# Turning the attention output: TensorE transposes against a DMA transpose of fp16 parts, with the batch loop written out

## The reference

```python
xn = layernorm(x)                                # over the 512 features
q, k, v = split(xn @ Wqkv.T + b)                 # 16 q, 8 k heads of 128; v in 4 groups of 256
p1 = softmax(causal(q[..., 0, :] @ k[..., 0, :].T / sqrt(128)))
p2 = softmax(causal(q[..., 1, :] @ k[..., 1, :].T / sqrt(128)))
o  = (p1 - lam * p2) @ v                         # 8 heads of 256 features
o  = o * rsqrt(mean(o * o) + 1e-5) * subln_w * (1 - 0.8 + 0.6 * exp(-0.3))
s  = concat(o) @ out_w.T + out_b                 # 2048 -> 512
g  = silu(mxfp4(xn) @ mxfp4(w_ffn).T + b_ffn)    # blocks of 32 rounded to 4 bits
out = x + s * g
```

## Time and profile before

| | |
|---|---|
| median of 3 runs | 1853.18 us (1851.12 to 1853.88) |
| profiled execution, span | 1849.4 us |
| PE busy | 1678.1 us (91%) |
| DVE busy | 1267.4 us (69%) |
| ACT busy | 965.0 us (52%) |
| POOL busy | 712.8 us (39%) |
| a batch of the loop (same piece of work, 839.0 less 623.35 us) | 215.65 us |
| data moved by DMA | 42.34 MB |

### The profile page before, as it was taken

One profiled execution on the slowest core, in us unless ns is written; L12 is line 12 of the kernel. 1 busy time (PEld: TensorE's weight loads), 2 busy tenths in 40 slices (PEclk: granted clock), 3 DMA queues, 4 the chain that ended last, 5 costly groups with the idle time before them and its releaser, 6 DMA issues.

```text
span 1849.4 us, 32092 instructions
## 1 busy us (share of the span) xinstructions
PE 1678.1 (91%) x10577; PEld 1036.1 (56%) x10577; DVE 1267.4 (69%) x2829; ACT 965.0 (52%) x2642; POOL 712.8 (39%) x1442
## 2 busy tenths in 40 slices
PE   3567999999899998999989998899989999999988
PEld 2344565556555565556655566555655566555654
DVE  4678888458864688548884588646885488844782
ACT  4655566336643466436663366435664356633661
POOL 2224553236422463225532364224632255323243
PEclk7879999999999999999999999999999999999999
DMA  7200000100000000100001000000001000000001
GB/s 256 91 24 1 1 2 5 48 18 2 1 30 29 13 1 1 42 24 7 1 14 41 18 1 1 30 24 18 1 1 42 24 7 1 7 24 24 1 1 40
DMA packets 20708, 42.34 MB, mean 23 GB/s; under 512 B 1682, under 2 KB 2228, under 8 KB 20532
## 3 DMA queue, kind: packets, MB, share of 16 engines
q1 hardware_dynamic: 20532, 40.13, 6.4%
HBM read 31.74 MB, written 8.39 MB: 22 GB/s over the span
## 4 chain that ended last, share of the span: by engine, by line
PE 40%; DVE 23%; issue 17%; ACT 11%; POOL 7%; DVEq 1%; DMA 0%; POOLq 0%; SPq 0%; ACTq 0%
PE ps L420 11%; PE ps L422 11%; PE ps L421 11%; ACT pp L656 7%; DVE negmax L924 5%; DVE qkv L881 2%; DVE ps L922 2%; DVE coef L937 2%; ACT qkv L634 2%; PE ps L476 1%; PE ps L544 1%; POOL res L1119 1%; DVE ebias L927 1%; DVE v L891 1%; POOL res L1122 1%
## 5 line engine op out<-in xcount | busy, mean ns | idle before, releaser
L656 ACT ACTIVATE pp<-ps,ebias,ssc 128x384 f32<-128x384 f32 (+3 forms) x512 | 312.1, 614 | 292.0 <-DVE ebias L927 225.5
L420 PE MATMUL ps<-xT,wqkv 128*128 128x512 f16 x768 | 296.0, 385 | 10.0 <-DVE qkv L881 5.9
L421 PE MATMUL ps<-xT,wqkv 128*128 128x512 f16 x768 | 295.6, 385 | 0.0
L422 PE MATMUL ps<-xT,wqkv 128*128 128x512 f16 x768 | 295.1, 384 | 0.0
L702 ACT ACTIVATE junk<-ps 128x256 bf16<-128x256 f32 x256 | 97.9, 383 | 274.7 <-PE ps L422 274.6
L420 PE MATMUL ps<-qkv,pT 128*128 128x256 f16 x640 | 174.4, 272 | 56.4 <-issue 40.4
L924 DVE TENSOR_REDUCE negmax<-ps 128x2 f32<-128x256 f32 (+3 forms) x256 | 211.1, 825 | 8.8
L913 DVE SCALAR_TENSOR_TENSOR res<-ps,small,obias 128x512 f32<-128x512 f32 x32 | 24.0, 751 | 255.5 <-PE ps L422 255.5
L420 PE MATMUL ps<-wout,heads 128*128 128x512 f16 x512 | 194.0, 379 | 0.0
L421 PE MATMUL ps<-wout,heads 128*128 128x512 f16 x512 | 194.0, 379 | 0.0
L422 PE MATMUL ps<-wout,heads 128*128 128x512 f16 x512 | 194.0, 379 | 0.0
(11 more groups left out here) (150 smaller groups left out, 3768.1 us busy)
## 6 DMA issues: line engine op xcount, KB each, us to landing
xin<-in_L_attn_hidden_states SPq DMA_DIRECT2D x8, 1024.0 KB, 5.4
xres<-in_L_attn_hidden_states SPq DMA_DIRECT2D x32, 256.0 KB, 2.8
out_x<-res SPq DMA_DIRECT2D x32, 256.0 KB, 2.1
qkv<-in_L_attn_Wqkv_w SPq DMA_DIRECT2D x8, 512.0 KB, 9.7
heads<-in_L_attn_Wqkv_w SPq DMA_DIRECT2D x8, 512.0 KB, 11.5
qkv<-in_L_attn_out_w SPq DMA_DIRECT2D x4, 512.0 KB, 4.0
heads<-in_L_attn_out_w SPq DMA_DIRECT2D x4, 512.0 KB, 3.6
gate<-in_L_ffn_weight SPq DMA_DIRECT2D x1, 1024.0 KB, 12.7
```

What stands on the lines that cost most here:

```text
L420: mm(out, ah, bh, start=start and j == 0, stop=False)
L421: mm(out, ah, bl, start=False, stop=False)
L422: last = mm(out, al, bh, start=False, stop=stop and j == n - 1)
L656: run(pp[:, m, 0:w], sc_ps[:, m, 0:w], ACT.Exp, bias=ebias[:, m:m + 1], scale=ssc[:, c:c + 1], accum_out=psum_l[:, s % 2, m:m + 1]).then_i ...
```

## The change

The attention output is split into its fp16 parts before it is turned, not after:

- `on` becomes fp16 with a high and a low part for each half. ACT's `normalised` writes the high part (256 elements, from PSUM, times the norm factor), after a wait until the DMA transpose has read this half two steps before.
- DVE's new `normalised_lo` writes the low part: o times the norm factor less the high part. It stands behind `combine` in every step. `heads_lo` goes.
- SP's new `transpose_o` issues one DMA transpose a step: the 128 x 512 fp16 of one half (2 blocks by 2 parts) go from `on` into `oT`, whose layout changes so that the parts of a block lie together. In group 0 it waits first until PE has read the old values. The stores and the residual loads are spread among the transposes in the same queue.
- PE's `transpose_o` and ACT's `heads_hi` go, and the PSUM bank `oT_ps`. PE's `attend` waits for both readers of `o_ps`. PE's output projection waits for the DMA semaphores of both halves.
- POOL's small tile `norm` gets two halves, and its last operation waits for `on_lo` of two steps before.
- `batches` runs all eight batches from a Python loop: the code of batches 1 to 6 is written out in place of the hardware loop.

```diff
-        oT = heads[:].bitcast(F16).rearrange("p (s c t) -> p s c t", s=2, c=OC)
+        oT = heads[:].bitcast(F16).rearrange("p (c s t) -> p c s t", s=2, c=OC)
-        on = sb("on", [P, 2, E], F32)
+        on = sb("on", [P, 2, 2, 2, P], F16)
-        norm = sb("norm", [P, 4], F32)
+        norm = sb("norm", [P, 2, 4], F32)
...
         def batches(eng, body):
-            body(Part(eng, 0, has_prev=False))
-            with eng.Fori(1, B - 1) as b:
-                body(Part(eng, b))
-            body(Part(eng, B - 1, has_next=False))
+            for b in range(B):
+                body(Part(eng, b, has_prev=b > 0, has_next=b < B - 1))
...
+            def transpose_o(g, r, step, h):
+                wait(sp, on_hi, step + 1)
+                wait(sp, on_lo, step + 1)
+                c = 4 * g + 2 * h
+                tok = slice(r // 2 * P, (r // 2 + 1) * P)
+                sp.dma_start_transpose(oT[:, c:c + 2, :, tok].rearrange("p c s t -> p (c s) t"),
+                                       on[:, h].rearrange("p c s t -> p (c s t)")).then_inc(oT_done[h], 16)
...
             def body(part):
+                for s in range(NS):
+                    g, r = s // STEPS, s % STEPS
+                    if s == 0:
+                        wait(sp, fill_done, part.fill0 - len(PROJ))
+                        wait(sp, q_done, part.blk0 + (NT + NT) if part.prev else NT)
+                        if part.next:
+                            sp.dma_start(xin[:], x_v[part.b + 1]).then_inc(ld_x, 16)
+                        if part.prev:
+                            residual(part.b - 1, 0)
+                    if part.prev and s in (2, 4, 6, 8):
+                        store(part.b - 1, s // 2 - 1, part.blk0 - NT)
+                        if s < 8:
+                            residual(part.b - 1, s // 2)
...
+                    if part.prev and g == 0 and r % 2 == 0:
+                        wait(sp, fill_done, part.fill0 + (part.order.index(("out", 0, r // 2)) + 1))
+                    transpose_o(g, r, part.step0 + s, s % 2)
...
-            def transpose_o(s, step):
-                h = s % 2
-                wait(pe, on_done, step + 1)
-                for e in range(2):
-                    last = tr(oT_ps[:, (2 * h + e) * P:(2 * h + e + 1) * P], on[:, h, e * P:(e + 1) * P], ident[:])
-                if h == 1:
-                    last.then_inc(oT_done, 1)
...
-            def normalised(s, step):
+            def normalised(s, step, sent):
                 wait(act, norm_done, step + 1)
-                run(on[:, s % 2, :], o_ps[s % 2], ACT.Copy, scale=norm[:, 2:3]).then_inc(on_done, 1)
-            def heads_hi(g, i, pair):
...
+                h = s % 2
+                wait(act, oT_done[h], sent)
+                run(on[:, h, :, 0, :], o_ps[h].rearrange("p (c t) -> p c t", c=2), ACT.Copy,
+                    scale=norm[:, h, 2:3]).then_inc(on_hi, 1)
...
-            def heads_lo(g, i, pair):
...
+            def normalised_lo(s, step):
+                h = s % 2
+                wait(dve, on_hi, step + 1)
+                stt(out=on[:, h, :, 1, :], in0=o_ps[h].rearrange("p (c t) -> p c t", c=2), scalar=norm[:, h, 2:3],
+                    in1=on[:, h, :, 0, :], op0=ALU.mult, op1=ALU.subtract).then_inc(on_lo, 1)
...
-                    if s % 2 == 0 and (s > 2 or part.prev):
-                        before = (s - 4) % NS
-                        heads_lo(before // STEPS, before % STEPS // 2, pair0 + (s // 2 - 2))
                     prepare_some(s, 0)
                     if more:
                         combine((s + 1) % STEPS, step + 1)
+                    if s or part.prev:
+                        normalised_lo((s - 1) % STEPS, step - 1)
                     prepare_some(s, 1)
```

More of the change, by code:

```diff
@@ L242, in build @@
         pT_ps = ps[:, 4, :]
-        oT_ps = ps[:, 5, :]
         o_ps = [ps[:, 6, 0:E], ps[:, 7, 0:E]]
@@ L287, in build @@
         norm_done = sem("norm_done")
[L288 to L292, removed]
+        on_hi = sem("on_hi")
+        on_lo = sem("on_lo")
+        oT_done = [sem(f"oT_done{h}") for h in range(2)]
         fill_done = sem("fill_done")
@@ L392, in store, with residual @@
+            def residual(batch, k):
+                sp.dma_start(xres[:], x_v[batch, :, k, :]).then_inc(ld_res, 16)
+            def store(batch, k, blk0):
                 wait(sp, summed, blk0 + k + 1)
-                sp.dma_start(out_v[part, :, k, :], res[:]).then_inc(res_free, 16)
+                sp.dma_start(out_v[batch, :, k, :], res[:]).then_inc(res_free, 16)
             def body(part):
-                wait(sp, fill_done, part.fill0 - len(PROJ))
-                wait(sp, q_done, part.blk0 + (NT + NT) if part.prev else NT)
@@ L400, in body @@
[L400 to L404, removed]
+                for s in range(NS):
[11 more added lines that the diff above has]
+                            residual(part.b - 1, s // 2)
+                    if not part.next and s == LAST_STEP:
+                        residual(part.b, 0)
+                    if not part.next and s == NS - 2:
+                        store(part.b, 0, part.blk0)
+                        residual(part.b, 1)
+                    if part.prev and g == 0 and r % 2 == 0:
+                        wait(sp, fill_done, part.fill0 + (part.order.index(("out", 0, r // 2)) + 1))
+                    transpose_o(g, r, part.step0 + s, s % 2)
@@ L406, in _ @@
             batches(sp, body)
-            for k in range(NT):
+            for k in range(1, NT):
+                if k > 1:
+                    residual(B - 1, k)
                 store(B - 1, k, (B - 1) * NT)
@@ L458, in fill @@
                     if first < OC - 4:
+                        if kind == "last":
+                            for h in range(2):
+                                pe.wait_ge(oT_done[h], ready - 16 * NT)
                         last = split3(bank, pairs[first:min(end, OC - 4)], start=first == 0, stop=False)
                     if end == OC:
-                        wait(pe, oT_lo, ready)
+                        for h in range(2):
+                            wait(pe, oT_done[h], ready)
                         last = split3(bank, pairs[OC - 4:], start=False)
@@ L493, in attend @@
                 wait(pe, pT_lo, step + 1)
-                wait(pe, on_done, step - 1)
+                wait(pe, on_hi, step - 1)
+                wait(pe, on_lo, step - 1)
                 v = vv[g % 2]
@@ L558, in body @@
                             wait(pe, fill_free, part.fill("aT", 0, j) + 1)
-                        ready = part.pair0 + (G - 1) * NT + j + 1 if kind == "last" else \
-                            part.pair0 - (NT - j - 1) if kind == "out" else 0
+                        ready = part.heads0 + 16 * ((G - 1) * NT + j + 1) if kind == "last" else \
+                            part.heads0 - 16 * (NT - j - 1) if kind == "out" else 0
                         fill(kind, gg, j, part.fill0 + local, local % 2, ready)
@@ L566, in body, with with_heads @@
                     attend(g, r, step)
[L567 to L574, removed]
+            def with_heads(part):
+                part.heads0 = part.step0 * 8 if isinstance(part.step0, int) else pe.snap(part.b * (NS * 8))
                 body(part)
-            batches(pe, with_pairs)
+            batches(pe, with_heads)
             n = len(PROLOGUE) + FILLS_0 + (B - 2) * FILLS_B + len(sum(schedule(True, False), []))
[L579 to L583, removed]
+            fill("out", 0, NT - 2, n, n % 2, B * NS * 8 - 16)
+            fill("out", 0, NT - 1, n + 1, (n + 1) % 2, B * NS * 8)
         @block.scalar
```

34 lines of the change are left out of this document (11 added, 23 removed).

## The result

The changed kernel takes 1880.12 us (median, 1879.24 to 1880.78) against 1853.53 us for the kernel before, timed beside it. The ratio is 1.0145, with a 95% interval of 1.0131 to 1.0160: slower by 1.4%. The forecast was 1863 us, +0.5%: the right sign, and a third of the size. The measured time stands at the upper end of the ring forecast's own range, 1845 to 1880. The profiled execution has a span of 1877.5 us, 28.1 us over the 1849.4 of the earlier trace rows; the forecast's sum said +9.8.

What follows compares the result with a forecast made beforehand. A ring through DVE and ACT bounds steps 8 to 31. Terms +33.6 (ring), +2 (batch 0), -6.6 (output), -5.0 (last batch), -14.2 (back edges) give +9.8 on 1849.4; median 3.8 higher, 1863 us; range 1815 to 1930, its own 1845 to 1880.

Steps and rivals of the forecast that it cites:

- ring forecast: Main case: DVE maxima, ACT exponentials, DVE combine and next fill set the pace in steps 8 to 31; 1863 us, chance 0.46.
- back edges: Five loop back edges where PE stands still 2.1 to 2.4 us and its clock drops; writing out saves 14.2 us.
- ring parts, six: Steps 8 to 31: new DVE operation +7.4, heads_lo and heads_hi removed -2.2, PE pairs -0.4; +4.8 us each.
- batch 0 (first): One ring part's +4.8 us, plus +2 us because steps 0 to 7 also quantise the weights on DVE.
- output parts, six: Steps 0 to 7, with the previous batch's projections: five of eight PE transpose pairs count, 1.1 us a batch, together -6.6 us.
- last batch: PE nearly always busy there, so removing its transpose pairs gives -5.0 us for the whole batch with its tail.
- Of 24 steps I take 19: Steps 8 to 31: the new DVE operation lengthens 19 by 0.39 us, +7.4 us a batch; the other five are free.
- if all 24 counted: Upper case for steps 8 to 31: the new DVE operation lengthens every step, +9.4 us a batch.
- The DMA transpose: One per step, SBUF to SBUF, taken as 4 us to landing; hidden, with 7.0 us free at the tightest place.
- Rival 1: Steps 8 to 31: removing L945 pays in full, 7.2 us, cancelling the new operation's 7.4; 1817 us, chance 0.28.
- Rival 2: DMA transposes landing after about 7 us or more make reuse of `on` set the pace; 1911 to 2100 us, chance 0.19.
- Rival 3: Writing out the loop only moves PE's standing still, a fetch, elsewhere: +14.2 us, 1877 us, chance 0.07.

Runs made afterwards that it cites:

- e1: The kernel before with its batch loop written out and nothing else changed: 1837.42 us, ratio 0.9917.
- e4: The kernel before, written out, with a DVE operation like the new one added behind combine and nothing removed: 1900.60 us, ratio 1.0258.
- e5: The kernel before, written out, with heads_lo 4 elements wide in the place of 512 from batch 1 on: 1831.99 us, ratio 0.9890.
- e7: The kernel before, written out, without PE's transposes of the output from batch 1 on: 1826.73 us, ratio 0.9867.
- e9: The kernel before, written out, with the added DVE operation only in steps 8, 15, 16, 17 and 24 of a batch: 1843.48 us, ratio 0.9956.
- e8: The kernel before, written out, operation added, heads_lo and heads_hi narrowed, PE's transposes dropped from batch 1 on, no DMA transposes: 1881.07 us, ratio 1.0157.
- e10: The changed kernel with each DMA transpose issued one step later: 1879.82 us, ratio 1.0153 to the kernel before.
- e2: The changed kernel with the low-part operation of step s-2 moved ahead of the low part of pT in step s: 1822.53 us, ratio 0.9832.
- e11: e2 with the attention output rotating over three PSUM banks and the low-part operation behind the low part of pT: 1817.61 us, ratio 0.9815.

## Why the prediction was right or wrong

The sum of the forecast, in spans, beside what the parts of the table give (after less e1; e1 less before for the loop). The last batch holds its output part, the piece from 8 to 30 and the tail:

| term | forecast | measured |
|---|---|---|
| back edges | -14.2 | -14.0 |
| ring parts, six | 6 x 4.8 = +28.8 | +38.6 |
| batch 0 (first) | 4.8 + 2 = +6.8 | +8.4 |
| output parts, six | -6.6 | -3.9 |
| last batch | -5.0 | -0.7 + 1.3 - 1.7 = -1.1 |
| sum (the spans differ by 28.1) | +9.8 | +28.0 |

**What bounds the kernel** was read rightly: e4, e5 and e7 show a ring through DVE and ACT in steps 8 to 31, and that DVE's added work costs the output parts nothing. This gave the sign, against a PE that is busy 91%. What failed is the price of two terms, and both sit where the operation was taken as free.

**The new operation in the ring part: the wrong step is that five of the 24 steps were held to be free.** "Of 24 steps I take 19" gave 7.4 us. By the starts of `combine` those 19 cost 7.1 us in e4, so this part of the term was good. The five that were left out, judged from the chain of the kernel before by the engine that had the piece behind `combine`, cost 1.15 us (e9). That chain could not show that a shift of 0.39 us makes `aq` 0.93 us longer. In six ring parts it is 7 us of the 18 missing. The forecast's own upper case ("if all 24 counted", +9.4 a ring part) would have given 1877 us.

**The last batch: no price for the operation at all.** The forecast put down only what PE and the tail gain, because PE was busy 148.65 of 149 us in 1616 to 1765. But that stretch begins before the last batch and ends before PE starts to wait: the piece from step 8 to 30 runs from 1693.4 to 1804.7, and in its last 40 us PE is busy 34.5 (columns as in the earlier trace rows):

```profile
1765.00:1804.70 39.70, 34.45 (x233) 21.54 (x231) 31.81 (x77) 25.45 (x75) 17.26 (x39) 1.00 0.00 1
```

e4's piece from step 8 to 30 is 4.4 us longer than e1's and its tail 0.4 shorter. PE's pairs gave 1.8 and 1.1 us there (e7), and 0.7 in the output part, not 5.3. "DVE's ring follows close behind" was said and not worked out. Together it is 3.9 us.

**The removals.** In the ring part `heads_lo` and `heads_hi` were put at 2.2 us and measured 0.9 + 0.8, with their narrow leftovers still there; PE's pairs at 0.4 and measured 0.65. One by one they come close to the forecast's 2.6 us, but beside the new operation all of them give only 161.1 - 159.0 = 2.1 us (e4 against e8, and against the kernel after): 3 us in six ring parts. The output part was put at 1.1 us and gave 0.65, 2.7 us in six. All these errors lie on the side that made the change look better. The rest is 1.6 us in batch 0 and 0.2 at the back edges.

**The DMA transpose** was put at 4 us and landed in 2.4; that it costs nothing up to 7 us is borne out by e8 and e10. By the Trainium skill, "VectorE: DVE Perf Modes", section "The three transpose paths", with its 1309 ns for one block, four blocks would take 5.2 us, an estimate; the profile after has all four within 2.4 us, to landing. The advice of the same page of the Trainium skill (section "Rules for kernel authors") to use TensorE where PSUM will do is not what decided here: e2 and e11 turn by DMA and are 15 and 20 us faster than e1, which turns on TensorE.

**The rivals.** Rival 1 (L945's removal cancels the operation) is refuted by e5: 0.9 us a ring part, not 7.2. Rival 2 (the DMA) by e8 and e10. Rival 3 (writing out saves nothing) by e1.

## What to carry to other kernels

When an engine has a high busy share but the chain of another stretch runs through a ring of two others, price an added operation on that ring at its start-to-start time in every step, also in the steps where the chain seems to leave the ring. Price what is removed beside it by what the chain gives back: here 2.1 us a ring part, of some 20 us of work taken off three engines. Then look for the pause inside the ring: here DVE waits for ACT between the bias and `combine`. Behind `combine` the operation makes the change 43 us slower than e1, with the loop written out in both; in that pause the same operation leaves it 15 us faster (e2), 20 us with three banks (e11). Against the kernel before these two are 1.7 and 1.9% faster, of which the written-out loop alone gives 0.8%. A change that frees a busy engine should be read together with where its replacement is put, since the place was worth 58 us and the transposes on PE only 11. And a small shift can cost more than its length where an operation on DVE meets one on POOL: compare durations before and after, not only waits.

## What the runs showed of the hardware

A DMA transpose of 128 x 512 fp16 from SBUF to SBUF lands 2.4 us after its issue in the median of 256, 4.7 us at the longest, about as a store of twice the bytes (2.3 us). SP's issue of it takes 1.19 us, against 0.34 for the store of the earlier trace rows and 0.57 for most stores of the kernel after. 256 of them beside the engines' work showed no cost (e8 against the kernel after, e10). At each of five back edges of the hardware loop PE stood still for 2.1 to 2.4 us, and writing the loop out gave 14.0 us for the five, with ring parts as long as the one that had no back edge. An operation of DVE on two SBUF tiles (`aq`) takes 0.68 us in most places and 1.77 us where it starts just behind an operation of POOL (L1121 in e9, L1114 in the kernel after).
